# Rotary halves of the queries: two blocks of four heads, one product, one addition, and transfers to their partitions

## The reference

```python
def _rope(x, L):
    x1, x2 = x[..., :half], x[..., half:]
    return concatenate([x1 * cos - x2 * sin, x1 * sin + x2 * cos])
kv_c = kv @ W_kvc                      # 64 numbers
q_c = layernorm(q) @ W_dq              # 96 numbers
q_nope, q_rope = q_c @ W_uq, _rope(q_c @ W_qr)     # 16 heads x 128, 16 heads x 64
k_nope, v = kv_c @ W_uk, kv_c @ W_uv
scores = (q_nope . k_nope + q_rope . _rope(kv_c @ W_kr)) * scale
attn = softmax(where(good, scores, NEG))
out = (attn @ v) @ W_o
# then x + gate * out, layer norm, quantised 256->1024, silu, gelu,
# layer norm, quantised 1024->256, and again a gated addition
```

## Time and profile before

| | |
|---|---|
| median of 3 runs | 251.46 us |
| profiled execution | 251.6 us |
| its span | 249.8 us |
| PE busy | 210.2 us (84%) |
| DVE busy | 187.7 us (75%) |
| ACT busy | 155.6 us (62%) |
| POOL busy | 149.7 us (60%) |
| scores(0) start | 37.13 us |
| scores(4), scores(8), scores(12) start | 54.29, 74.13, 93.04 us |
| scores(16) to scores(28), each tile | 22.1 us |

### The profile page before, as it was taken

How to read it: one execution, slowest core, us unless ns; L and a number is a source line. 1 busy time by engine, 2 the same in 40 slices (tenths; PEclk the granted TensorE clock), 3 DMA queues, 4 the chain that set the end, 5 groups by cost and what they waited for, 6 DMA issues and landing times.

```text
span 249.8 us, 4518 instructions
## 1 busy us (share of the span) xinstructions
PE 210.2 (84%) x1452; PEld 167.5 (67%) x1452; DVE 187.7 (75%) x430; ACT 155.6 (62%) x455; POOL 149.7 (60%) x222
## 2 busy tenths in 40 slices
PE   1799899999999999998998999899899746834453
PEld 1677788688978877886786888678678632513231
DVE  2587556689786679988988998898899842779761
ACT  2256627737557597759559875965887593849021
POOL 0415726639776469788787878778787832062630
PEclk9999999999999999999999999999999996775557
DMA  6999994000000000000000000000000000000001
GB/s 194 286 213 184 318 385 189 0 0 3 1 3 0 3 3 0 3 0 0 24 1 0 25 0 0 4 21 0 4 22 0 3 0 21 0 0 0 24 22 31
DMA packets 11357, 12.40 MB, mean 50 GB/s; under 512 B 3936, under 2 KB 10336, under 8 KB 11104
## 3 DMA queue, kind: packets, MB, share of 16 engines
q1 hardware_dynamic: 10432, 11.44, 16.6%
q10 hardware_dynamic: 896, 0.61, 0.8%
HBM read 11.00 MB, written 1.05 MB: 48 GB/s over the span
## 4 chain that ended last, share of the span: by engine, by line
PE 45%; DVE 19%; POOL 12%; issue 11%; ACT 9%; DMA 1%; DVEq 0%; SPq 0%; POOLq 0%
PE bank_pair L805 7%; PE bank_score L883 5%; PE bank_ff L920 4%; POOL h_small L430 4%; PE bank_lat L907 4%; PE bank_swap L808 3%; DVE z L1206 3%; PE bank_prob L895 3%; DVE h L1230 3%; POOL prob_room L485 3%; DVE neg_max L1289 3%; ACT prob_room L654 3%; PE bank_ff L959 3%; PE bank_ff L939 2%; POOL qcat L408 2%
## 5 line engine op out<-in xcount | busy, mean ns | idle before, releaser
L654 ACT ACTIVATE prob_room<-bank_score,neg_max 128x128 f32<-128x128 f32 x128 | 45.3, 369 | 23.5 <-DVE neg_max L1289 23.5
L485 POOL TENSOR_TENSOR prob_room<-prob_room,rsum 128x512 f32<-128x512 f32 x32 | 33.3, 1041 | 26.0 <-DVE rsum L1297 25.8
L406 POOL TENSOR_TENSOR qcat<-qcat,turned 64x256 f32<-64x256 f32 x32 | 30.8, 963 | 11.9 <-DVE turned L1141 11.8
L883 PEld LDWEIGHTS bank_score<-kcat,qcat 128*128 128x128 f32 x256 | 33.7, 192 | 2.3
L805 PE MATMUL bank_pair<-qcT,wcat 96*128 96x128 f32 x256 | 34.0, 276 | 0.0
L883 PE MATMUL bank_score<-kcat,qcat 128*128 128x128 f32 x256 | 33.7, 275 | 0.0
L642 ACT COPY probT_room<-bank_prob 128x512 f32<-128x512 f32 x32 | 19.0, 594 | 22.4 <-PE bank_prob L895 22.4
L920 PE MATMUL bank_ff<-m_sb,latT 128*128 128x256 f32 x128 | 31.9, 395 | 0.0
L805 PEld LDWEIGHTS bank_pair<-qcT,wcat 96*128 96x128 f32 x256 | 31.1, 192 | 0.4 <-DVE wcat L1126 0.2
L408 POOL TENSOR_TENSOR qcat<-qcat,turned 64x256 f32<-64x256 f32 x32 | 29.6, 924 | 2.5
L1137 DVE TENSOR_TENSOR qcat<-bank_pair,cst 128x512 f32<-128x512 f32 x32 | 21.6, 674 | 10.5 <-PE bank_swap L808 10.5
(11 more groups left out here) (163 smaller groups left out, 436.6 us busy)
## 6 DMA issues: line engine op xcount, KB each, us to landing
wo<-in_L_xattn_W_o SPq DMA_DIRECT2D x1, 2048.0 KB, 19.5
w_sb<-in_L_ffn_w SPq DMA_DIRECT2D x2, 1024.0 KB, 9.9
out_x<-y SPq DMA_DIRECT2D x8, 128.0 KB, 1.7
wuq<-in_L_xattn_W_uq SPq DMA_DIRECT2D x1, 768.0 KB, 11.5
ctx_all<-in_ctx ACTq DMA_DIRECT2D x2, 256.0 KB, 5.0
x_all<-in_x SPq DMA_DIRECT2D x2, 256.0 KB, 4.7
cst<-in_consts SPq DMA_DIRECT2D x1, 512.0 KB, 7.0
x_all<-in_x SPq DMA_DIRECT2D x1, 512.0 KB, 8.2
```

Source lines behind the costliest of these rows:

```text
L406: nc.gpsimd.tensor_tensor(odd, odd, add_odd, ALU.add).then_inc(pair_half, 1)
L485: nc.gpsimd.tensor_tensor(p, p, rsum[:, k % 2, :].unsqueeze(2).broadcast_to([P, GROUP, kts * P]), ALU.mult).then_inc(prob_scaled, 1)
L654: last = nc.scalar.activation(prob_of(n, kts)[:, j, :], src[:, j, :], ACT.Exp, bias=neg_max[:, k % 2, j:j + 1], accum_out=esum[:, k % 2, j ...
L883: last = nc.tensor.matmul(bank[:, j * kts * P:(j + 1) * kts * P], qcat[:, k, hh // 2, hh % 2, :], kcat[:, b, hh % 2, 0:kts * P], start=Fal ...
```

## The change

The rotary parts of the four heads of a step are no longer projected to the partitions on which `qcat` needs them. `wrope` has two blocks for each step: the first halves of four heads (4 x 32 = 128 rows) and the second halves. Two products make both (L855 of the new file, into `bank_swap`), one DVE operation multiplies them with four tables (cosine, minus sine, sine, cosine) into `product`, and one POOL addition over 128 partitions gives `rotated`. Eight transfers of 32 partitions x 128 numbers (16 KB each), issued by SP, put these rows where `qcat` has them. The folded parts are two more products (L860, two heads each, into `bank_pair`), and ACT copies them to `qcat` by two copies of 64 partitions (`copy_nope`). So PE has four products to a step instead of six. AHEAD is 3 instead of 2. W_qr is loaded by one transfer into the room of `tanh_z` instead of two into `wcat`; the table of constants that is loaded grows by 2 x 256 columns.

```diff
-AHEAD = 2
+AHEAD = 3
-EYE, IOTA, COS, SIN, CONSTS = 0, P, P + S, P + 3 * S, P + 4 * S
+EYE, IOTA, ROT, SIN, CONSTS = 0, P, P + S, P + 5 * S, P + 6 * S
@@ SP
-            load(wcat[:, :, 0, KVC:P], wqr_pair[:, :, 0, :], "wqr0")
-            load(wcat[:, :, 1, 0:R], wqr_pair[:, :, 1, :], "wqr1")
+            load(wqr[:, :], W_qr, "wqr")
...
-            for f in range(F):
-                sp.wait_ge(y_done, f + 1)
-                sp.dma_start(out_v[f, :, :], y[:, :]).then_inc(out_stored, 16)
+            def move_rope(n):
+                k = n % STEPS
+                sp.wait_ge(rope_rotated, n + 1)
+                if n >= STEPS:
+                    sp.wait_ge(score_ready, n - STEPS + 1)
+                for hh in range(GROUP):
+                    for o in range(2):
+                        lo = (KVC if hh % 2 == 0 else 0) + o * half_r
+                        sp.dma_start(qcat[lo:lo + half_r, k, hh // 2, hh % 2, :],
+                                     rotated[hh * half_r:(hh + 1) * half_r, k, o, :]).then_inc(rope_moved[k], 16)
+            for n in range(N):
+                move_rope(n)
+                c = (n - 4 * STEPS - AHEAD) // STEPS
+                if c >= 0 and n == c * STEPS + 4 * STEPS + AHEAD:
+                    store(c)
+            for c in range((N - 1 - 4 * STEPS - AHEAD) // STEPS + 1, F):
+                store(c)
@@ POOL, add_rope_step
-                add_rope(qcat[KVC:P, k, :, 0, :], qcat[0:R, k, :, 1, :], t[KVC:P, :, :], t[0:R, :, :], B + step_no(f, k))
+                pool.wait_ge(rope_multiplied, n + 1)
+                if f > 0:
+                    pool.wait_ge(rope_moved[k], MOVED * f)
+                nc.gpsimd.tensor_tensor(rotated[:, k, :, :], product[:, k % 2, :, 0, :], product[:, k % 2, :, 1, :],
+                                        ALU.add).then_inc(rope_rotated, 1)
@@ ACT
+            def copy_nope(f, k):
+                n = step_no(f, k)
+                act.wait_ge(nope_ready, n + 1)
+                if f > 0:
+                    act.wait_ge(score_ready, n - STEPS + 1)
+                nc.scalar.copy(qcat[0:KVC, k, :, 0, :], src[0:KVC, :, :])
+                nc.scalar.copy(qcat[KVC:P, k, :, 1, :], src[KVC:P, :, :]).then_inc(nope_copied, 1)
...
-                        if f < F:
-                            exponentials(f, k, kts)
+                        exponentials(f, k, kts)
+                        if step_no(f, k) + AHEAD < N:
+                            copy_nope(*ahead(f, k))
@@ PE, project
-                pe.wait_ge(pair_turned, s)
-                for j in range(2):
-                    for e in range(2):
-                        nc.tensor.matmul(bank_pair[:, (2 * j + e) * P:(2 * j + e + 1) * P], wcat[:, 2 * k + j, e, :], src, ...)
-                for j in range(2):
-                    last = nc.tensor.matmul(bank_swap[:, j * P:(j + 1) * P], wswap[:, 2 * k + j, :], src, ...)
+                pe.wait_ge(rope_multiplied, n)
+                for e in range(2):
+                    last = nc.tensor.matmul(bank_swap[:, e * P:(e + 1) * P], wrope[:, k, e, :], src, ...)
+                last.then_inc(rope_ready, 1)
+                pe.wait_ge(nope_copied, n)
+                for j in range(2):
+                    last = nc.tensor.matmul(bank_pair[:, j * P:(j + 1) * P], wnope[:, 2 * k + j, :], src, ...)
+                last.then_inc(nope_ready, 1)
@@ PE, scores
-                pe.wait_ge(pair_done, B + n + 1)
+                pe.wait_ge(nope_copied, n + 1)
+                pe.wait_ge(rope_moved[k], MOVED * (f + 1))
@@ DVE, turn_step
-                nc.vector.tensor_tensor(qcat[:, k, :, :, :], bank_pair[:, :].rearrange(...), cos, ALU.mult)
-                nc.vector.tensor_tensor(turned[:, k % 2, :]..., bank_swap[:, 0:S]..., sin, ALU.mult)
+                nc.vector.tensor_tensor(product[:, k % 2, :, :, :], x, rot_tab[:, :, :, at:at + P],
+                                        ALU.mult).then_inc(rope_multiplied, 1)
```

88 lines of the change are left out of this document (52 added, 36 removed).

## The result

The kernel before takes 251.94 us (median of 4 runs made beside the new one), the changed kernel 261.02 us (259.76 to 261.65, 4 runs): a ratio of 1.034, 95% interval 1.027 to 1.042. Forecast were 255.1 us and a range of 249 to 259. The direction was right; the time lies beyond the range.

A forecast was written before the change was run, and what follows sets the result against it. PE was taken to bound tiles 1 and 2, with DVE, POOL, ACT and PE in turn later. 251.6 + 6.4 (start) + 2.7 (clock) - 4.9 (PE) + 0 (late tiles) - 0.7 (step (7, 1)) = 255.1 us, range 249 to 259.

The forecast's parts named there:

- In these tiles ACT has 4 to 8 us free in a tile, and I cost it at nothing: Tiles 0 to 2: project's new wait for ACT's copy of the step before was put at 0 us.
- -4.9 for PE: Tiles 0 to 2: two products fewer save 0.45 us a step over 11 steps, -4.9 us.
- +2.7 for the clock: From scores(0): PE starts at 1.2 GHz after an idle gap, +2.7 us; 0 to +3.5.
- each step loses up to one pair of copies: Tiles 0 to 2: if ACT's free time gives no cover, up to 0.74 us a step.
- Late tiles, predicted 0 from -7.4 to +3.3: Tiles 3 to 7: ACT's added copies use up the relief of DVE and POOL, 0 us.
- The chain that I had followed: Tile 5's waits: exponentials, tanh, silu, POOL, probability copies; ACT's copies (+0.74 a step) would use up POOL's gain.
- The start, predicted +6.4: Before scores(0): eight transfers wait behind all weight loads on SP, scores(0) at 43.5, +6.4 us.
- Rival 2: scores(0): loads do not hold the transfers, start at 39.6, +2.5 instead of +6.4, total 248.5 us; chance 0.11.
- The gate's 19.1 us: Earlier trace: a 0.5 KB load landed 19.1 us after its issue began, taken as evidence that small transfers wait behind loads.
- The transfers later on, predicted as hidden, 0 us: Steps after the start: about 3 us of SP issues in a 5.5 us step, landing before scores needs them, 0 us.
- Step (7, 1), -0.7: Step (7, 1) has neither project, copy nor addition; DVE's 0.72 us wait for POOL goes, -0.7 us.
- Rival 4: Late tiles: ACT becomes the bound, or SP's issues are longer; +0.74 a tile, +3.3, total 258.4 us; chance 0.10.

The follow-up runs named there:

- no_moves: Changed kernel without its 256 transfers, rotary rows of qcat set to one at the start and nobody waiting for them; 251.94 us, ratio 1.001.
- idle_copies: no_moves with ACT's copies reading a constant and writing spare rows, nobody waiting for them; 253.25 us, ratio 1.007.
- no_moves_no_copies: Changed kernel without the transfers and without ACT's two copies a step, all of qcat set to one; 238.24 us, ratio 0.948.
- before_copies: Kernel before with two idle ACT copies of 64 x 256 added after the exponentials of each of 29 steps; 257.89 us, ratio 1.023.
- four_moves: Changed kernel with four transfers of 64 partitions a step instead of eight of 32, same bytes, rows landing wrongly; 254.27 us, ratio 1.014.
- moves_first: Changed kernel with the loads of b1, ln_g, ln_b and b2 issued behind the transfers of steps 0 to 2; 259.60 us, ratio 1.030.
- kept_busy: Changed kernel with 30 useless 128x128 products on PE ahead of scores(0); 256.27 and 260.02 us, ratio 1.025.
- both_halves: Changed kernel with four transfers a step, a head's rotary rows interleaved, the reference's output kept; 255.97 us, ratio 1.018.
- best4: Changed kernel with both_halves' transfers, even heads' copy on DVE, loads of b1, ln_g, ln_b, b2 behind the first transfers; 249.63 us, ratio 0.993.
- two_steps: Changed kernel with each transfer carrying two steps, 128 transfers instead of 256, same bytes; 270.35 us, ratio 1.075.
- dve_one_copy: no_moves with the even heads' copy made by DVE behind its product, the odd heads' by ACT; 247.57 us, ratio 0.984.

## Why the prediction was wrong

The starts of the steps split the spans of the traces into stages, in us. Each column is one kernel, and the two kernels between differ by one part each:

| stage | before | neither part | with copies (no_moves) | with transfers (after) |
|---|---|---|---|---|
| to scores(0) | 37.1 | 38.0 | 37.5 | 44.7 |
| scores(0) to (12) | 55.9 | 52.7 | 58.6 | 60.1 |
| scores(12) to (31) | 105.2 | 94.5 | 102.8 | 103.7 |
| to the end | 51.6 | 51.4 | 50.5 | 50.5 |
| span | 249.8 | 236.5 | 249.5 | 259.0 |

**The step that failed: "In these tiles ACT has 4 to 8 us free in a tile, and I cost it at nothing".** The copies cost 5.9 us between scores(0) and scores(12). The sum had -4.9 for PE there; without the copies the stage is 3.2 us shorter, and with them 2.7 us longer than before. The stage as a whole came out at +4.2 us, where its terms (-4.9 for PE, +2.7 for the clock) made -2.2. Of these 6.4 us the copies are 5.9, 1.7 are relief that did not come, and -1.2 is the clock (1.5 for 2.7, below). As to the relief, PE's busy time in the stage fell from 55.02 to 49.59 us, and PE stood still for 3.1 us of it instead of 0.9. Free time of an engine on average covers work only where nobody waits for what stands behind it. no_moves in tile 0, first the timeline, then stretches of it:

```profile
45.64 0.37 ACT L612 COPY qcat<-bank_pair 64x256 f32<-64x256 f32 x1
...
46.03 1.91 ACT L627 ACTIVATE w2q<-w_sb 128x2048 bf16<-128x2048 f32 x1
...
48.05 0.58 ACT L682 COPY probT_room<-bank_prob 128x512 f32<-128x512 f32 x1
...
48.69 0.69 PE L956 MATMUL bank_lat<-probT_room,kvc 128*64 128x256 f32 x4 [1.68 <-ACT probT_room L682]
49.17 3.58 PE L890 MATMUL bank_ff<-wo,h 128*64 128x256 f32 x16
```

```profile
46.00:49.00 3.00, 1.32 (x14) 1.06 (x14) 1.19 (x3) 2.95 (x7) 1.72 (x2) 1.00 0.00 0
49.00:53.00 4.00, 3.76 (x20) 1.80 (x16) 0.89 (x2) 2.02 (x9) 0.00 (x0) 0.57 0.00 0
```

ACT works without a pause there. Two pairs of copies have pushed the copy of the probabilities back by 1.5 us, to 48.05 from 46.56 without them; PE waits 1.68 us, where the kernel without copies has this:

```profile
47.23 0.65 PE L948 MATMUL bank_lat<-probT_room,kvc 128*64 128x256 f32 x4 [0.65 <-ACT probT_room L679]
...
49.00:53.00 4.00, 3.11 (x28) 2.65 (x25) 3.19 (x6) 0.55 (x1) 0.00 (x0) 1.00 0.00 0
```

The wait is 1.0 us longer, and behind it the granted clock is 0.57 and not 1.00: 16 products (L890) take 3.58 us, where the same 16 take 1.90 without the copies. Step 2 lasts 9.46 us instead of 6.74. That is 2.7 of the 5.9 us, of which 1.7 went through the clock. Whether the wait made the clock fall is not shown. In idle_copies PE waits longer at the same place, and the clock stays:

```profile
48.35 0.65 PE L952 MATMUL bank_lat<-probT_room,kvc 128*64 128x256 f32 x4 [2.31 <-ACT probT_room L681]
...
46.00:49.00 3.00, 0.69 (x7) 0.49 (x8) 0.32 (x1) 3.00 (x8) 1.32 (x2) 1.00 0.00 0
49.00:53.00 4.00, 3.12 (x28) 2.26 (x25) 2.31 (x5) 1.75 (x8) 0.00 (x0) 1.00 0.00 0
```

The alternative was in the text, "each step loses up to one pair of copies", 0.74 us, 8 us for these tiles, and had no chance of its own.

**Late tiles, predicted 0 from -7.4 to +3.3: right in sum by luck, both sides larger.** From scores(12) to scores(31), first the kernel before, then no_moves_no_copies, then no_moves:

```profile
93.04:198.22 105.18, 98.53 (x719) 80.48 (x717) 95.13 (x209) 75.80 (x243) 83.19 (x118) 1.00 0.02 6
90.70:185.15 94.45, 88.16 (x634) 71.79 (x638) 85.64 (x189) 75.73 (x243) 62.81 (x97) 1.00 0.02 7
96.14:198.96 102.82, 91.91 (x635) 74.79 (x638) 84.45 (x186) 89.09 (x281) 61.96 (x97) 0.97 0.02 7
```

The relief is 10.7 us, and ACT's copies give 8.4 of it back. The chain that I had followed, from the exponentials over the copies and tanh to silu, is there: DVE's silu waits for tanh in the changed kernel, and no such wait is listed for the kernel before. These are the waits (us in all, times, the longest) of the changed kernel, and below them those of no_moves_no_copies:

```profile
DVE z L1263 <- ACT tanh_z L653: 8.9, 6, 2.2
...
DVE z L1248 <- ACT tanh_z L643: 3.5, 6, 1.4
```

But the bounds were too narrow. The lower one was DVE's own time, and took nothing off for PE, whose busy time falls by 10.4 us in these tiles (98.53 to 88.16) as DVE's falls by 9.5; which of the two the 10.7 us are, no run separates. The copies cost 0.44 us a step of the 0.73 put there, and that too is partly the clock: 0.97 over 102.82 us is at most 3 us of PE's work. before_copies gives 7.4 us for the same stage, by itself.

**The start, predicted +6.4: measured +7.6, of which the transfers are 7.2.** The place was right, the reason half. I put the transfers behind the loads' backlog alone, and that gave 43.5. The eighth transfer is issued at 38.8, 4.4 us behind the first, and lands 5.8 us later, where the median of all is 1.8: about 4 us are the backlog and as much the seven issues ahead of it. four_moves, with four issues fewer in the same place, starts 2.8 us earlier, and moves_first, without the four loads, 4.3 us earlier. Rival 2's 39.6 was wrong because its issues were too short and because there is a backlog: even with all four loads moved away it was 40.43. The gate's 19.1 us, which I had set against this rival, were for 12.56 us its own issue; what was left, 6.5 us, is what the first transfer took here.

**The transfers later on, predicted as hidden, 0 us: wrong.** The prediction had "Eight issues of 0.33 to 0.43 us are about 3 us of SP in a step that lasts 5.5". They take 0.63 us from start to start, 5.1 a step and 20.3 in a tile of 22. The waits of PE for them in the changed kernel, in all, times, longest:

```profile
PE bank_score L935 <- DMA qcat<-rotated: 11.4, 5, 7.2
```

7.2 of the 11.4 us are the start, the other four waits come from scores(8) on. Those of steps 1 to 4 land 1.0 to 3.7 us ahead of their scores, so that a start earlier than this is soon lost again: moves_first and kept_busy won 4.3 and 1.5 us in step 0, and by scores(4) had 0.1 and 0.3 of it. With four issues a step the start is kept (both_halves), and best4 has scores(4) at 55.39. In the table the transfers cost 7.2 us ahead of scores(0), 1.5 up to scores(12), which is also what the clock took in step 0, and 0.9 after it.

The Trainium skill (DMA: Bandwidth & Descriptors, Rules for kernel authors) has small transfers gathered into large ones. The runs agree in direction, and give the reason here: halving the number of issues at equal bytes (both_halves) gave back 5.0 of 9 us, while a landing stayed at 1.8 to 1.9 us. The prediction weighed this rule by the landings, found that they overlap, and left the sum alone; the issues did not overlap, 46 of them took 29.83 us.

**The clock, predicted +2.7: measured about 1.5.** The fall to 0.50 and its place were right (stretches above); step 0 lasts 3.48 us and 1.99 with a busy PE. The return came by 48 us, after about 3.3 us of work, where the earlier trace rows had about 5. By scores(4) 0.3 us of it was left. What the prediction left out is that the clock also fell in later tiles: from scores(12) to scores(31) it was 0.97, where the kernel before had 1.00.

**Step (7, 1), -0.7**: from scores(29) to scores(30) it takes 5.71 us instead of 6.25, so -0.5. No run looks at it alone.

Rival 4 named both causes, "ACT becomes the bound of the late tiles, or SP's issues turn out longer", and put them at 258.4 with a chance of 0.10. What came was both at once, and the net of it at the start and in the early tiles: in the late tiles ACT's copies cost more than that rival's 3.3 us, and the relief more than paid for them.

What stays open: how the copies' price divides between early and late tiles. no_moves pays 5.9 and 8.4 us, idle_copies, whose copies take 0.40 us, 4.0 and 10.7. The early difference is nearly the 1.7 us that the clock took in step 2 of no_moves and not of idle_copies; the late one no run explains. What makes the clock fall in some tiles is open too. Two banks for the products, so that PE runs ahead of the copies, were not tried, nor was a second engine that issues half of the transfers in every step.

## What to carry to other kernels

Count the issues of a queue as you count instructions of an engine, with a duration from an issue of the same kind, and compare issues times duration with the length of a step; here 256 small transfers filled SP, and an earlier start, or a kept clock, was gone by scores(4) as long as there were eight a step. Work moved onto an engine with free time is free only if nothing that others wait for is queued behind it: ask what stands right behind the new instruction, and price it at full size in the range if it is a copy that the bound engine needs. When an exchange between engines comes to nothing, leave out each side by itself: here that showed a gain of 13 us and a price of 13.7 us behind a difference of near zero.

## What the runs showed of the hardware

- An issue of 32 partitions x 512 bytes within SBUF takes SP 0.59 us (median of 256), 0.63 from start to start; one of 32 partitions x 1 KB (both_halves, two_steps) or of 64 x 512 bytes (four_moves) takes 0.60, while the last load of a broadcast vector takes 0.43. Between these transfers the number of bytes and of pieces makes hardly a difference. The earlier trace rows did not show this kind of issue.
- A copy of 64 partitions x 256 takes ACT 0.36 to 0.37 us from PSUM (no_moves) and 0.40 to 0.41 us from SBUF (idle_copies, before_copies); DVE takes 0.41 us for the same copy from PSUM (dve_one_copy).
- In no_moves a wait of 1.68 us of PE was followed by a granted clock of 0.57, in idle_copies one of 2.31 us at the same place by 1.00, and so was one of 0.65 us in no_moves_no_copies. So a wait of about this size may be followed by the half clock or not; no run shows what decides.
- Small transfers within SBUF, issued behind the weight loads, took up to 6.5 us to land, where the median is 1.8 us; with the last four loads (1.6 MB) moved behind them the eighth took 2.1 us instead of 5.8 (moves_first).
